# Closing norm of a state-space layer: batch 0 moved into the loop's run-out, batch 1 into the next block

## The reference, cut to what matters

```python
x = x + _layernorm(_L1_attn_ref(_layernorm(x), ...))   # the state-space layer
x = x + _layernorm(_L1_ffn_ref(_layernorm(x), ...))    # the per-head MLP

def _layernorm(x, axis=-1, eps=1e-05):
    m = jnp.mean(x, axis=axis, keepdims=True)
    v = jnp.var(x, axis=axis, keepdims=True)
    return (x - m) / jnp.sqrt(v + eps)

# per-head MLP: permute channels, 32 -> 128 per head, gelu, 128 -> 32, permute back
t = t[:, perm].reshape(b * l, h, d)
t = jnp.einsum('bhd,hdm->bhm', t, up)
t = jax.nn.gelu(t, approximate=False)
t = jnp.einsum('bhm,hmd->bhd', t, down).reshape(b * l, h * d)[:, unperm]
```

## Time and profile before

| stretch of the trace, us | what runs | busy |
|---|---|---|
| 0 to 2592 | three layers, and the loop's steady part | PE 9 tenths and more in most slices |
| 2592 to 2638.5 | the loop's run-out, batch 1 | waits between engines |
| 2638.8 to 2656.2 | closing block | DVE alone, with POOL at its side |
| 2657.9 to 2665.6 | the head's statistics | DVE |
| 2665.6 to 2739.5 | the head's MLP, last norm, stores | PE, then DVE |

### The profile page before, as it was taken

The page is one execution under the profiler, slowest core; times in us unless marked ns, Lnnn a source line. Parts: engine busy times, 40 slices in busy tenths (PEclk is TensorE's granted clock), DMA queues, the critical chain, the costliest instruction groups (busy, mean ns, idle before and its releaser), DMA issues. The chain is left out here.

```text
span 2739.5 us, 37352 instructions
## 1 busy us (share of the span) xinstructions
PE 2503.8 (91%) x12664; PEld 1824.7 (67%) x12664; DVE 1751.1 (64%) x3146; ACT 1414.4 (52%) x2794; POOL 1509.2 (55%) x1299
## 2 busy tenths in 40 slices
PE   7989995899699779999999999999999999999948
PEld 3464443444487568878878877877877877877734
DVE  2053454576433767777777777777777777777764
ACT  2200003555221376676676676686676776776603
POOL 0053465454001238668668667677667777767641
PEclk9999998899799989999999999999999999999978
DMA  4012320000210253343342342342342352342210
GB/s 159 0 49 69 107 62 31 1 1 1 85 61 13 84 160 104 93 148 96 101 148 95 102 148 89 104 151 89 103 153 89 94 161 88 95 157 90 71 46 31
DMA packets 143483, 241.86 MB, mean 88 GB/s; under 512 B 28352, under 2 KB 48576, under 8 KB 143168
## 3 DMA queue, kind: packets, MB, share of 16 engines
q1 hardware_dynamic: 143296, 239.48, 27.7%
HBM read 232.08 MB, written 7.34 MB: 87 GB/s over the span
## 5 line engine op out<-in xcount | busy, mean ns | idle before, releaser
L1670 ACT ACTIVATE mix<-mix,sc 128x128 f32<-128x128 f32 x1024 | 310.9, 389 | 6.1 <-DMA sc<-head_scal 3.1
L98 PE MATMUL ps<-xt_hi,w_in_hi 128*128 128x512 f32 x640 | 269.6, 421 | 34.0 <-ACT sg L1660 29.6
L1840 DVE SCALAR_TENSOR_TENSOR feat<-ps,chan,feat 128x511 f32<-128x511 f32 (+2 forms) x384 | 284.1, 740 | 7.0 <-ACT feat L1650 5.3
L1988 POOL TENSOR_TENSOR w_in_lo<-w_in_raw,w_in_hi 128x512 fp32r<-128x512 f32 x158 | 213.3, 1350 | 135.1 <-ACT w_in_hi L1625 135.1
L1874 DVE TENSOR_TENSOR y_lo<-y,y_hi 128x512 fp32r<-128x512 f32 x128 | 174.9, 1366 | 159.7 <-ACT y_hi L1686 157.6
L1829 DVE TENSOR_TENSOR mix<-mix,cb 128x512 f32<-128x512 f32 x256 | 273.8, 1074 | 0.0
L1972 POOL TENSOR_TENSOR xend<-xdt,sc 128x384 f32<-128x384 f32 x128 | 107.3, 838 | 290.9 <-DVE xdt L1803 289.1
L99 PE MATMUL ps<-xt_lo,w_in_hi 128*128 128x512 f32 x640 | 256.0, 400 | 0.0
L100 PE MATMUL ps<-xt_hi,w_in_lo 128*128 128x512 f32 x640 | 255.7, 400 | 0.0
L98 PE MATMUL ps<-xt_hi,w_g_hi 128*128 128x512 f32 x512 | 214.9, 420 | 22.9 <-DVE feat L1840 22.9
L1517 PE MATMUL ps<-w_o_hi,y_hi 128*128 128x512 f32 x512 | 207.4, 405 | 5.1 <-DVE y_lo L1874 3.4
(11 more groups left out here) (270 smaller groups left out, 5975.9 us busy)
## 6 DMA issues: line engine op xcount, KB each, us to landing
mix<-row_cum SPq DMA_DIRECT2D x128, 512.0 KB, 5.7
w_in_raw<-in_w_conv_in SPq DMA_DIRECT2D x160, 256.0 KB, 3.2
w_g_raw<-in_w_gate_in SPq DMA_DIRECT2D x128, 256.0 KB, 3.3
ecb<-row_ecum SPq DMA_DIRECT2D x256, 96.0 KB, 3.3
w_o_raw<-in_w_out SPq DMA_DIRECT2D x64, 256.0 KB, 3.0
w<-in_w_c2q SPq DMA_DIRECT2D x16, 768.0 KB, 4.6
w<-in_w_c2q SPq DMA_DIRECT2D x16, 512.0 KB, 3.7
wqkv<-in_w_qkv SPq DMA_DIRECT2D x1, 3072.0 KB, 13.6
```

Of the source, the lines that this page charges most:

```text
L98: pe.matmul(out, a_hi, b_hi, start=(n == 0), stop=False)
L1670: last = act.activation(m, m, ACT.Relu, bias=sc[:, b, CUM, z, 2 * i + e:2 * i + e + 1], scale=-1.0)
L1840: dve.scalar_tensor_tensor(out=to, in0=ps[:, j % 2, 0:S - back], scalar=chan[:, bb % B, j, K1 - 1 - back:K1 - back], in1=to, op0=ALU.mult, ...
L1988: pool.tensor_tensor(w_in_lo[:, n % RING, :, :], w_in_raw[:, n % RING, :, :], w_in_hi[:, n % RING, :, :].bitcast(F32), ALU.subtract).then_ ...
```

## The change

The closing block is removed. In the run-out VectorE and GpSimd norm batch 0's four tiles of acc, add the old x and take the statistics for the head's norm. SyncE loads the old x at step 0 of the run-out, 1 MB for each batch, into the tiles w_in_raw and w_in_hi, which have no more use after the last projection. Batch 1's four tiles are normed, added and measured in the head's block, between the steps of batch 0. The head's order is changed with it: the gather matrix comes after batch 0's tiles, the turns of batch 1 come in steps 2 and 3, two in each, before and behind the step's `up` and `down`, and `down` has one PSUM bank.

```diff
-    def stage_end(self):
-        self.nc.clear_and_free_semaphores(self.sems)
+    def stage_end(self, alive=()):
+        self.nc.clear_and_free_semaphores([s for s in self.sems if s not in alive])
         self.nc.all_engine_barrier()
...
             def loads(sp, g, b, k):
+                if not main and k == 0:
+                    wait(sp, "proj_ready", g, 0, 0)
+                    for bn in range(B):
+                        sp.dma_start(st.x_old[bn], st.x_saved[:, bn * ZB:(bn + 1) * ZB, :]).then_inc(st.x_back, 16)
...
             def on_vector(dve, g, b, k):          # at the end of each step
+                if not main and k == 1:
+                    for t in range(ZB):
+                        dve.bn_stats(core.stats[:, t, :], acc[:, t, :]).then_inc(st.fin.stats, 1)
+                if not main and k == 2:            # bn_aggr x4, then vare
+                if not main and k == 4:
+                    dve.wait_ge(st.fin.rstd, 1)
+                    for t in range(ZB):            # tensor_scalar, in place
+                if not main and k == 5:
+                    dve.wait_ge(st.x_back, 16 * B)
+                    for t in range(ZB):            # x = acc + old x
+                if not main and k == 6:            # bn_stats x4 of x
+                if not main and k == 7:            # bn_aggr x4, then vare
...
             def on_pool(pool, g, b, k):            # at the end of the step
+                if not main and k in (3, 8):
+                    pool.wait_ge(st.fin.vare, 1 + k // 8)
+                    pool.tensor_tensor(core.rstd[:, 0:ZB], core.vare[:, 0:ZB], core.half[:, 0:ZB], ALU.pow).then_inc(st.fin.rstd, 1)
...
-        with ExitStack() as inner:                 # the closing block, L2091 to L2126
...
 head_mlp, VectorE:
+                dve.wait_ge(st.fin.rstd, 2)
                 norm(0)
                 norm(1)
                 for t in range(HALF):
                     low(t)
-                    norm(t + 2)
-                for t in range(HALF):
-                    keep_xp(t)
-                    low(HALF + t)
-                    if HALF + t + 2 < NT:
-                        norm(HALF + t + 2)
+                    if t + 2 < HALF:
+                        norm(t + 2)
+                gather_matrix()
+                last_measured()        # bn_stats x4, bn_aggr x4, vare of acc, tiles 4 to 7
+                keep_xp(0)
+                last_added()           # wait for the root, scale x4, add tiles 4 and 5
+                keep_xp(1)
+                half_measured()        # bn_stats x4, bn_aggr x4, vare of x
+                norm(HALF)
+                norm(HALF + 1)
+                keep_xp(2)
+                low(HALF)
+                norm(HALF + 2)
+                cut_z(0)
+                low(HALF + 1)
+                norm(HALF + 3)
+                keep_xp(3)
+                low(HALF + 2)
+                cut_z(1)
+                low(HALF + 3)
...
 head_mlp, GpSimd, at its start:
+                # root for last_added; add tiles 6 and 7; root for norm(4) to norm(7)
...
 head_mlp, ScalarE and TensorE, in the loop over steps:
-                    if step < HALF:
-                        turn(HALF + step)
+                    if step in LATE_TURNS:         # {2: (4, 5), 3: (6, 7)}
+                        turn(LATE_TURNS[step][0])
                     if 1 <= step <= NB:
                         up(step - 1)
                     if step >= 2:
                         down(step - 2)
+                    if step in LATE_TURNS:
+                        turn(LATE_TURNS[step][1])
...
                 def down(j):
-                    if j == 1:
-                        pe.wait_ge(xt_lo_done, NT)
-                    if j >= 2:
-                        pe.wait_ge(z_done, j - 1)
+                    if j >= 1:
+                        pe.wait_ge(z_done, j)
```

More of the change, by code:

```diff
@@ L172, in __init__, with all @@
         self.added = core.sem(name + "_added")
+    def all(self):
+        return [self.stats, self.aggr, self.vare, self.rstd, self.scaled, self.added]
 def add_vector(dve, core, s, t, src, scaled):
@@ L2088, in _, with head_mlp @@
                     groups(pool, on_pool)
-        with ExitStack() as inner:
[L2092 to L2129, removed]
+def head_mlp(core, st, w_up2, w_down2, perm, c_iota, out):
     nc, ps, x = core.nc, core.ps, core.x
@@ L2196, in _ @@
             def _(dve):
[L2197 to L2211, removed]
+                late = range(HALF, NT)
+                def gather_matrix():
+                    dve.wait_ge(perm_loaded, 48)
+                    dve.tensor_copy(perm_rowf[:, :], perm_row[:, :]).then_inc(perm_float, 1)
+                    dve.tensor_copy(perm_colf[:, :], perm_col[:, :]).then_inc(perm_float, 1)
+                    dve.wait_ge(perm_float, 1)
+                    for k in range(KD):
+                        dve.tensor_scalar(take[:, k, :], perm_rowf[:, :], iota[:, D + k:D + k + 1], None,
+                                          ALU.is_equal).then_inc(take_done, 1)
@@ new lines, in spread, with last_measured @@
+                def spread(sems, turn):
+                    for i, t in enumerate(late):
+                        dve.wait_ge(sems.stats, turn * HALF + i + 1)
+                        dve.bn_aggr(core.mv[:, t, :], core.stats[:, t, :]).then_inc(sems.aggr, 1)
+                    dve.wait_ge(sems.aggr, turn * HALF + HALF)
+                    dve.tensor_scalar(core.vare[:, HALF:], core.mv[:, HALF:, 1], LN_EPS, None, ALU.add).then_inc(sems.vare, 1)
+                def last_measured():
+                    for t in late:
+                        dve.bn_stats(core.stats[:, t, :], x[:, t, :]).then_inc(st.fin.stats, 1)
+                    spread(st.fin, 2)
@@ new lines, in last_added @@
+                def last_added():
+                    dve.wait_ge(st.fin.rstd, 3)
+                    for t in late:
+                        dve.tensor_scalar(x[:, t, :], x[:, t, :], core.mv[:, t, 0:1], core.rstd[:, t:t + 1],
+                                          ALU.subtract, ALU.mult).then_inc(st.fin.scaled, 1)
+                    for t in (HALF, HALF + 1):
+                        dve.wait_ge(st.fin.scaled, t + 1)
+                        dve.tensor_tensor(x[:, t, :], x[:, t, :], st.x_old[1][:, t - HALF, :], ALU.add).then_inc(st.fin.added, 1)
@@ L2213, in norm, with half_measured @@
+                def half_measured():
+                    for t in late:
+                        dve.wait_ge(*((st.fin.added, t + 1) if t < HALF + 2 else (late_added, t - HALF - 1)))
+                        dve.bn_stats(core.stats[:, t, :], x[:, t, :]).then_inc(ln.stats, 1)
+                    spread(ln, 0)
                 def norm(t):
-                    if t == 0:
+                    if t == HALF:
                         dve.wait_ge(ln.rstd, 1)
@@ L2318, in _ @@
                 for step in range(NB + 2):
-                    if step < HALF:
-                        keep_turned(HALF + step)
+                    if step in LATE_TURNS:
+                        keep_turned(LATE_TURNS[step][0])
                     if 1 <= step <= NB:
@@ L2324, in _ @@
                         high(step - 2)
+                    if step in LATE_TURNS:
+                        keep_turned(LATE_TURNS[step][1])
             @blk.tensor
@@ L2496, in program @@
             state_space(core, st, *pick("w_conv_in w_gate_in w_out1 chan_wb norm_w c_keep"))
-        core.stage_end()
-        head_mlp(core, *pick("w_up2 w_down2 perm c_iota"), out)
+            core.stage_end(st.fin.all())
+            head_mlp(core, st, *pick("w_up2 w_down2 perm c_iota"), out)
 def kernel(**inputs):
```

52 lines of the change are left out of this document (40 added, 12 removed).

## The result

The changed kernel takes 2729.18 us (median of 5 runs, 2725.43 to 2732.02) against 2742.55 us; the ratio is 0.9948, 95% interval 0.9934 to 0.9961. That is 13.4 us less, in the direction forecast but more, and under the lower end of the range, 2731. In a later comparison the same pair gave 2730.41 and 2740.85 us, ratio 0.9963 (0.9950 to 0.9975), 10.4 us less.

A forecast was written before the change was run, and what follows sets the result against it. TensorE was taken to bound nearly the whole span, so gain had to come from its standstill at the seam. Terms: -25.4 + 6.4 (run-out) + 2.1 + 8.2 + 1.5 = -7.2 us, giving 2735.4 us; range 2731 to 2741.

The forecast's parts named there:

- term 1: Seam: without closing block and up-front statistics, `norm(0)` follows `accumulate` after one stage change; -25.4 us.
- term 2: Run-out: four statistics on VectorE ahead of `with_dt(7)` delay TensorE's `inside(7)`; +1.7 us.
- term 3: Run-out: TensorE's wait of 3.1 us before `inside(7)` lowers its clock for the products behind; +1.6 us.
- term 4: Run-out: GpSimd's root of 128x4 delays `finish(7)` and what hangs on it; +1.0 us.
- term 5: Run-out: VectorE's scales, adds and statistics between `low(7)` and `mean` exceed its idle 5.50 us; +2.1 us.
- term 6: Head: the gather matrix, formerly beside the root, now delays `gather(0)`; +2.1 us.
- term 7: Head, `gather(0)` to `gather(4)`: batch 1's norm, add and statistics chain lengthens it to 26.4 us; +8.2 us.
- term 8: Head: TensorE's 2.4 us wait for `low(7)` lowers the clock for `gather(4)` and what follows; +1.5 us.
- A: Rival: neither the 3.1 nor the 2.4 us TensorE wait lowers the clock; -10.3, 2732.3 us; chance 0.22.
- B: Rival: batch 1's chain and the run-out, with VectorE-GpSimd hand-overs, cost 3 to 5 more; 2739.5 us; chance 0.18.
- C: Rival: VectorE and GpSimd hinder each other on SBUF, dearer adds and scales; 2743.3 us, slower; chance 0.05.
- D: Rival: the 2 MB transfers come late and put 7.8 us on the run-out; 2743.2 us; chance 0.03.

The follow-up runs named there:

- busy: Changed kernel plus nine matmuls nobody reads in TensorE's wait ahead of `inside(7)`; 2730.86 us against 2742.74 for the kernel before.
- early: Changed kernel with batch 0's statistics and root moved to the end of run-out step 0, scales ahead of `low(6)`; 2727.50 us against 2740.85 before.
- behind: Changed kernel with batch 0's norm, addition and statistics in one piece behind the last `accumulate`; 2738.80 us, ratio 0.9988 to the kernel before.
- before_end: Kernel before plus seven matmuls nobody reads in TensorE's wait ahead of `give_back(2)`; 2740.93 us, ratio 0.9991 to the kernel before.

## Why the prediction was right and wrong

| step | forecast, us | in the profiled pair | how it shows |
|---|---|---|---|
| term 1, closing block and statistics gone | -25.4 | -25.3 | `accumulate` to `norm(0)` 27.12, now 1.81 |
| term 2, statistics ahead of `with_dt(7)` | +1.7 | +1.6 | `low(4)` to `with_dt(7)` 2.15, now 3.75 |
| term 3, the clock fell | +1.6 | +1.6 | 5.43, now 7.01; busy: 5.43 |
| term 4, root ahead of `finish(7)` | +1.0 | +1.0 | L2079 1.02, no wait on either side |
| term 5, work ahead of `mean` | +2.1 | +2.0 | `low(7)` to `mean` 6.47, now 8.46 |
| term 6, gather matrix uncovered | +2.1 | +2.0 | `norm(0)` to `gather(0)` 7.26, now 9.22 |
| term 7, batch 1's chain | +8.2 | +8.0 | 18.17, now 26.19 |
| term 8 and the rest of the head | +1.5 | -0.9 | `gather(4)` to the end 48.4, now 47.5 |
| sum | -7.2 | -10.2 | `low` of step 0 to the end 139.0, now 128.9, the terms within 0.1; with 0.2 more between load and run-out, -10.4 |

**What failed is term 8**, "the clock falls, and `gather(4)` and what follows lose 1.5". The wait was there, 2.36 us for 2.4, but the clock stayed at 1.00 in both traces of the changed kernel, and the 1.5 us were not lost. Among six traces with this same wait it fell in two (early and busy), at 1.6 us each. I made a sure cost of a chance of about one in three. The rest of that row is a gain that I did not price: the old kernel's clock at `give_back(2)` was low in both its traces with the wait (5.2 and 5.4 us up to `give_back(3)`), and high in eight of nine of the new ones (4.0), behind the same wait of 1.9. That is another 1.2 us; why it stays up there is open. `down` in one bank, priced at 0, took 0.3 back.

**Term 7 came out right partly by luck.** From `gather(0)` to `turn(4)` it took 12.9 us where I had 14.25, and from `turn(4)` to `gather(4)` 13.3 where I had 12.15. The wait at `turn(4)` was 3.47 and not 5.2. The four scales and two adds on VectorE took 3.1 and not 4.6, and three of the four second statistics ran beside GpSimd's adds, which ended last; I had put all four behind. Against that, `up(1)` and `down(0)` at the lower clock took 3.9 and not 2.8.

**The other 3 us of the medians are not shown at the seam.** The first comparison gave 13.4 us, its repetition 10.4, and the traces 10.4 in both. The 10.4 alone would have been 2732.2, inside the range of 2731 to 2741. The range allowed for the steps and not for what lies ahead of them, which moved by 7 us over the traces; three runs within 2.5 us had made it look steady. Where the 3 us lie stays open: of the first five executions only the shortest has a trace, and without it their median would still be 2729.3.

**Rivals.** A, the clock holds (2732.3, chance 0.22), was nearest: right for term 8, wrong for term 3. The wait of 1.91 us at 2723.16 that spoke for it was no fair witness, as the clock was at 0.50 already in the 2 us ahead of it. The rule of the Trainium skill, "TensorE: Matmul & The Clock Gate", section "What's actually happening", as the prediction used it, would have had terms 3 and 8 at 0. The traces agree with it at the wait of 2.36 to 2.37 us in four of six, and not in the other two, nor behind the 2.94 to 2.95 of `inside(7)` in any of four. B: nearly all hand-overs between `norm(0)` and `gather(4)` took 0.02 to 0.07 us, one 0.30. C: the price is real (4.29 us for four scales in early), but `square(7)` had ended at 2628.53, 1.6 us ahead of the first add of step 5, and the four took 2.48. D: the load was issued at 2578.6 and landed within 8.2 us, over 40 ahead of the adds; in behind the run-out is 38.03 with it.

## What to carry to other kernels

Moving work into the waits of a pipeline's run-out is worth what the gap of that very engine at that very place holds: the same 12.3 us of work cost 12.3 behind the loop, 6.1 in gaps picked roughly, and 0.9 in gaps picked from the idle column of the timeline. Before a matmul that waits for a late chain, put everything in TensorE's queue that doesn't; here `gather(0)` to `gather(4)` got 3.2 us shorter by it, with 2.1 us of later work done besides, though some 2 us were lost again at a lower clock near the end of that kernel's one trace. Compare two traces from an anchor behind the part that scatters, and price a clock fall behind a wait of some 2 us as a chance, counted over several traces at that very place, not as a term.

## What the runs showed of the hardware

- The granted clock behind a wait of TensorE that began at full clock, from the run-out to the end, over the twelve traces: it never fell behind 1.29 to 1.60 us (31 waits). Ahead of `give_back` it fell behind 4 of 20 waits of 1.91 to 1.92, ahead of an `inside` in the run-out behind 11 of 12 waits of 1.99 to 2.00, ahead of `project(7)` (L1517 to L1519) behind all four of 2.06 to 2.08 and one of two of 2.31, ahead of `gather(4)` behind 2 of 6 of 2.36 to 2.37. It fell behind each of the 17 waits of 2.94 to 4.08. So between 1.9 and 2.4 us the place counted for more than the length.
- Filling the wait of 2.95 us ahead of `inside(7)` kept the clock up there (busy, one trace). Filling one wait in the old kernel moved the fall to the next one (before_end, one trace).
- VectorE's 128x512 scale from SBUF takes 0.48 us alone (behind) and 1.07, the mean of four, beside GpSimd's `finish` and `square` (early). Its statistics of one such tile take 0.61 alone and with GpSimd busy beside two of four (changed).
- GpSimd's two adds in the head took 2.74 us beside VectorE's fourth scale and two adds, and 1.27 beside VectorE's statistics; in the closing block before, four of them took 1.43 to 1.64, beside VectorE's scales and its first add.
- Attention, unchanged in all kernels, ended at 719.5 to 719.8 us in two traces and at 724.1 to 726.5 in ten; TensorE's granted clock from 480 to 600 us goes with it.
